# Starting the first expert pass with six early 256-token blocks

## The reference, cut to what matters

```python
scores = (jnp.einsum('btd,ed->bte', x, router_w) + router_b) / temp
gates = _sinkhorn(scores)
topk_vals, topk_idx = jax.lax.top_k(gates, K)
g = jax.nn.relu(jnp.einsum('btd,edf->btef', x, wg))
p = jnp.einsum('btd,edf->btef', x, wp)
all_out = jnp.einsum('btef,efd->bted', g * p, wo)
...
x = L0_attn_x
x = x + _L0_attn_ref(xn, ...) + _L0_ffn_ref(xn, ...)
```

## Time and profile before

| what | value |
|---|---|
| median of three runs | 388.4 us (387.77 to 388.95) |
| span of the profiled execution | 387.7 us |
| TensorE busy | 346.6 us |
| GpSimd busy | 267.4 us |
| mean granted TensorE clock | 0.982 |

### The profile page before, as it was taken

One profiled execution on the slowest core, in us unless ns is written; L12 is line 12 of the kernel. 1 busy time (PEld: TensorE's weight loads), 2 busy tenths in 40 slices (PEclk: granted clock), 3 DMA queues, 4 the chain that ended last, 5 costly groups with the idle time before them and its releaser, 6 DMA issues.

```text
span 387.7 us, 8994 instructions
## 1 busy us (share of the span) xinstructions
PE 346.6 (89%) x2632; PEld 311.0 (80%) x2632; DVE 271.5 (70%) x745; ACT 235.4 (61%) x442; POOL 267.4 (69%) x363
## 2 busy tenths in 40 slices
PE   0779799799989888999999999999999999999880
PEld 0769568667768777786699999999999999999770
DVE  3998789998798888774266666676656666666440
ACT  3679644126756655653268777777767777775530
POOL 3696999947877544647065777777756777777773
PEclk9999999969999999999999999999999999999996
DMA  6999999997424323259467677677674555563330
GB/s 181 253 315 334 336 334 266 319 248 225 137 100 146 116 82 98 94 157 310 112 170 191 191 214 210 183 223 212 174 207 116 160 135 164 140 170 106 93 103 0
DMA packets 64287, 70.98 MB, mean 183 GB/s; under 512 B 6099, under 2 KB 59103, under 8 KB 64241
## 3 DMA queue, kind: packets, MB, share of 16 engines
q1 hardware_dynamic: 53968, 48.56, 47.6%
q0 software_dynamic: 8672, 21.19, 15.0%
q10 hardware_dynamic: 1600, 0.67, 0.7%
HBM read 28.54 MB, written 43.04 MB: 185 GB/s over the span
## 4 chain that ended last, share of the span: by engine, by line
PE 68%; DVE 16%; issue 6%; POOL 4%; DMA 3%; ACT 2%; SPq 0%; ACTq 0%; POOLq 0%; DVEq 0%
PE psum L1652 15%; PE psum L1639 7%; PE psum L1640 7%; PE psum L1641 7%; PE psum L1617 4%; PE psum L1459 3%; PE psum L1521 3%; PE psum L1629 3%; POOL out L551 3%; PE psum L1350 2%; DVE stats L844 2%; PE psum L1441 2%; DMA rows<-in_L_attn_x 2%; PE psum L1403 2%; PE psum L1444 2%
## 5 line engine op out<-in xcount | busy, mean ns | idle before, releaser
L537 POOL DMA_INDIRECT by_upper<-row x70 | 69.0, 985 | 35.0 <-issue 15.1
L529 POOL DMA_INDIRECT by_lower<-rows,slot_u x64 | 64.5, 1008 | 36.0 <-DVE rows L960 19.2
L551 POOL DMA_INDIRECT out<-row x70 | 68.8, 983 | 25.7 <-issue 15.9
L1652 PE MATMUL psum<-w_expert,hT 128*128 x560 | 76.9, 277 | 1.0 <-DVE hT L1283 0.5
L1639 PE MATMUL psum<-xT_high,w_now 128*128 128x256 f32 x232 | 70.2, 303 | 0.8 <-issue 0.8
L1652 PEld LDWEIGHTS psum<-w_expert,hT 128*128 128x128 f32 x560 | 69.4, 192 | 1.8 <-issue 1.6
L748 ACT ACTIVATE w_now<-w_split 128x1024 fp32r x58 | 61.4, 1058 | 15.4 <-PE psum L1641 15.4
L1641 PE MATMUL psum<-xT_high,w_now 128*128 128x256 f32 x232 | 65.5, 282 | 0.0
L1640 PE MATMUL psum<-xT_low,w_now 128*128 128x256 f32 x232 | 65.4, 282 | 0.0
L1287 DVE TENSOR_TENSOR hT<-relu,psum 128x512 f32<-128x512 f32 x58 | 39.9, 687 | 34.7 <-PE psum L1641 31.3
L1295 DVE SCALAR_TENSOR_TENSOR row<-psum,row 128x128 f32<-128x128 f32 x140 | 43.6, 346 | 9.6 <-PE psum L1652 1.5
(11 more groups left out here) (256 smaller groups left out, 697.4 us busy)
## 6 DMA issues: line engine op xcount, KB each, us to landing
by_lower<-blank SPq DMA_DIRECT2D x1, 10140.0 KB, 34.8
by_upper<-blank SPq DMA_DIRECT2D x1, 10062.0 KB, 72.7
row<-by_lower SPq DMA_DIRECT2D x29, 260.0 KB, 3.4
row<-by_upper SPq DMA_DIRECT2D x29, 258.0 KB, 3.1
rows<-in_L_attn_x SPq DMA_DIRECT2D x8, 512.0 KB, 9.5
row<-by_upper SPq DMA_DIRECT2D x12, 129.0 KB, 2.2
row<-by_lower SPq DMA_DIRECT2D x11, 130.0 KB, 2.4
by_upper<-row POOLq DMA_INDIRECT x70
```

Source lines behind the costliest of these rows:

```text
L529: pool.indirect_dma_start(by_lower, bass.IndirectOffsetOnAxis(ap=slot_u[:, t:t + 1], axis=0), rows[:, t, :], None).then_inc(scattered, 16)
L537: pool.indirect_dma_start(by_upper, bass.IndirectOffsetOnAxis(ap=row[:, q, k, SLOT_UP:SLOT_UP + 1].bitcast(U32), axis=0), row[:, q, k, 0:R ...
L551: pool.indirect_dma_start(out_rows, bass.IndirectOffsetOnAxis(ap=row[:, q, k, TOKEN:TOKEN + 1].bitcast(U32), axis=0), row[:, q, k, BASE], ...
L1652: last = pe.matmul(psum[:, 4 + n % 2, k * D:(k + 1) * D], hT[:, n % 3, f, k * P:(k + 1) * P], weights, start=(f == 0), stop=(f == FB - 1))
```

## The change

Pass one starts with six pairs (LEAD = 6), then come the 12 singles, then the other 23 pairs. SP may load one of the six as soon as the scatters of the first 52 tiles (SOON) have landed, if the block lies wholly in them by a table (`lead_need` is 1), and otherwise when all 64 have (`lead_need` is 2). GpSimd counts this in the semaphore `arrived`. The table is computed on VectorE: three more instructions in `pair_bounds`, one in `class_bounds`, the new `lead_waits` of seven in iteration 10, one in `entry_numbers`. The ring changes places with w_whole, xT_low and relu, so that rows can be loaded during the attention's last groups and w_whole can't; SP's order is now: load_expert(1) to (6), six row loads, both copies of w_whole (once the last output chunk is through), the row loads 6 to 9, load_expert(7), the rest. The fillers go, round and divide of expert 6 stand before the attention's last instructions, those of expert 7 in blocks 20 and 21, and a register load is made for each word of packed numbers when it is first needed.

```diff
+    LEAD = 6
+    SOON = 52
+    FIRST_PASS = [*range(LEAD), *range(PAIRS, NE), *range(LEAD, PAIRS)]
+    def listed(n):
+        return FIRST_PASS[n] if n < NE else n - NE
     def width(n):
-        return 1 + ((n % NE >= SINGLES) if n < NE else (n % NE < PAIRS))
-    def listed(n):
-        return (n + PAIRS) % NE if n < NE else n - NE
+        return 1 + (listed(n) < PAIRS)
...
             w_now = last_use("w_now", [P, 2, 4 * FF], F32R)
-            w_whole = last_use("w_whole", [P, E, 2 * FF])
+            row = last_use("row", [P, NB, 2, ROW])
...
-        LAST_BANKS = (6, 7, 0, 1)
+        LAST_BANKS = (6, 7, 3, 4)
...
+        def pack_reader(engine):
+            packs = {}
+            def expert(a, i):
+                at = listed(a * NE + i)
+                k = a * NPACK + at // PACK
+                if k not in packs:
+                    _, (packs[k],) = nc.values_load_multi_w_load_instructions(packed_no[:, k:k + 1], ...)
+                return (packs[k] >> (3 * (at % PACK))) & (E - 1)
+            return expert
...  SP, load_row and the queue
                 if n == 0:
-                    sp.wait_ge(scattered, 16 * NT)
+                    sp.wait_ge(q_ready, NG - 1)
+                if n < LEAD:
+                    sp.wait_ge(arrived, sp.value_load(lead_need[:, n:n + 1], min_val=1, max_val=2))
+                if n == LEAD:
+                    sp.wait_ge(arrived, 2)
...
-            sp.wait_ge(q_ready, NG)
+            sp.wait_ge(route_dve, TABLES_STEP)
+            for n in range(LEAD):
+                load_row(n, by_lower, ROW)
+            sp.wait_ge(o_chunk, G)
             sp.dma_start(w_whole[:, :, 0:FF], wg.rearrange("e p f -> p e f")).then_inc(whole_loaded, 16)
             sp.dma_start(w_whole[:, :, FF:2 * FF], wp.rearrange("e p f -> p e f")).then_inc(whole_loaded, 16)
-            sp.wait_ge(o_chunk, G)
-            load_expert(E - 1)
-            sp.wait_ge(route_dve, TABLES_STEP)
-            for n in range(NE):
+            for n in range(LEAD, NE):
+                if n == LEAD + 4:
+                    load_expert(E - 1)
                 load_row(n, by_lower, ROW)
...  GpSimd
-                                            rows[:, t, :], None).then_inc(scattered, 16)
+                                            rows[:, t, :], None)\
+                        .then_inc(scattered_soon if t < SOON else scattered_late, 16)
+                    if t == SOON:
+                        pool.wait_ge(scattered_soon, 16 * SOON)
+                        pool.sem_inc(arrived, 1)
+            pool.wait_ge(scattered_late, 16 * (NT - SOON))
+            pool.sem_inc(arrived, 1)
...  ScalarE
-            round_expert(E - 2)
+                if n == NG - 2:
+                    round_expert(E - 2)
...
+                        if n + 4 == LEAD:
+                            act.wait_ge(whole_loaded, 32)
...  VectorE
+            def lead_waits():
+                soon_to = bounds[:, 2, 0]
+                link(dve.tensor_tensor(soon_len[:], soon_to[:, 1:], soon_to[:, 0:K], ALU.subtract))
+                link(dve.tensor_tensor(soon_end[:], pairs_to[:, 0, 0:K], soon_len[:], ALU.add))
+                link(dve.tensor_tensor(soon_more[:], soon_end[:, 1:], soon_end[:, 0:K - 1], ALU.subtract))
+                link(dve.tensor_tensor(lead_part[:], in_later[:, 0, 0:LEAD], soon_more[:]..., ALU.mult))
+                link(dve.tensor_reduce(lead_sum[:], lead_part[:], AX_X, ALU.add))
+                link(dve.scalar_tensor_tensor(lead_late[:], lead_sum[:], soon_end[:, 0:1], pair_at[:, 0:LEAD],
+                                              ALU.add, ALU.is_le))
+                link(dve.tensor_scalar(lead_need[:], lead_late[:], 1.0, None, ALU.add))
...
-                link(dve.tensor_scalar(need_no[:], need[:], pair_end[:, 0:1], float(SINGLES), ALU.add, ALU.add))
+                link(dve.tensor_scalar(need_first[:], need[:], pair_end[:, 0:1], float(LEAD), ALU.add, ALU.max))
+                link(dve.tensor_scalar(need_no[:], need_first[:], float(SINGLES), None, ALU.add))
...
+            divide_expert(E - 2)
             for c in range(G):
                 finish_last(c)
-            divide_expert(E - 2)
...  TensorE
-            unread(36)
-            pe.wait_ge(scattered, 16 * NT)
-            unread(13)
```

More of the change, by code:

```diff
@@ L171, in sparse_block_kernel @@
         before_wide = sb("before_wide", [K2, 2, K + 1])
-        wide = sb("wide", [K2, 2, 2, K + 1], BF16)
+        wide = sb("wide", [K2, 3, 2, K + 1], BF16)
+        soon_sum = sb("soon_sum", [K2, 1], I32)
+        soon_no = sb("soon_no", [K2, 1], I32)
+        soon_f = sb("soon_f", [K2, 1])
+        soon_len = sb("soon_len", [1, K])
+        soon_end = sb("soon_end", [1, K])
+        soon_more = sb("soon_more", [1, K - 1])
+        lead_part = sb("lead_part", [1, LEAD, K - 1])
+        lead_sum = sb("lead_sum", [1, LEAD])
+        lead_late = sb("lead_late", [1, LEAD])
+        lead_need = sb("lead_need", [1, LEAD], I32)
         pair_sum = sb("pair_sum", [K2, 1], I32)
@@ L235, in sparse_block_kernel @@
             rden = first("rden", [P, G])
-        row = sb("row", [P, NB, 2, ROW])
+        xT_low = sb("xT_low", [P, 2, W], F32R)
+        relu = sb("relu", [P, 2, FB * W])
         hT = sb("hT", [P, 3, FB, W])
+        w_whole = sb("w_whole", [P, E, 2 * FF])
         psum = ctx.enter_context(nc.psum_tensor("psum", [P, 8, 512], F32))
         x_in = [sem(f"x_in{b}") for b in range(B)]
-        (v_loaded, w_loaded, const_ready, lower_cleared, upper_cleared, scattered) = steps(
-            "v_loaded w_loaded const_ready lower_cleared upper_cleared scattered")
+        (v_loaded, w_loaded, const_ready, lower_cleared, upper_cleared, scattered_soon, scattered_late, arrived) = steps(
+            "v_loaded w_loaded const_ready lower_cleared upper_cleared scattered_soon scattered_late arrived")
         (rw_loaded, rw_pe, rw_step, w_scaled, w_summed, w_sum_saved, w_step) = steps(
@@ L337, in turn_of @@
             return n // NB + 1
-        def load_numbers(engine, ap, top):
-            _, numbers = nc.values_load_multi_w_load_instructions(
-                ap, engines=[engine], min_val=0, max_val=top, bass_reorder=False,
-                skip_runtime_bounds_check_because="eight class numbers below 8 in base 8")
-            return numbers
+        def pack_reader(engine):
[4 more added lines that the diff above has]
+                if k not in packs:
+                    _, (packs[k],) = nc.values_load_multi_w_load_instructions(
+                        packed_no[:, k:k + 1], engines=[engine], min_val=0, max_val=E ** PACK - 1, bass_reorder=False,
+                        skip_runtime_bounds_check_because="eight class numbers below 8 in base 8")
+                return (packs[k] >> (3 * (at % PACK))) & (E - 1)
+            return expert
         block = ctx.enter_context(nc.Block())
@@ L789, in _ @@
                     n = n0 + i
-                    if a == 0 and i == 6:
+                    if a == 0 and i == LEAD + 14:
                         round_expert(E - 1)
@@ L1235, in divide_expert @@
                    .then_inc(w_divided, 1)
-            TABLES = {5: class_lengths, 6: pair_places, 8: single_places, 9: choose_singles, 11: entry_numbers}
+            TABLES = {5: class_lengths, 6: pair_places, 8: single_places, 9: choose_singles, 10: lead_waits, 11: entry_numbers}
             for n in range(EARLY, NG):
@@ L1304, in _ @@
                     n = n0 + i
-                    if a == 0 and i == 7:
+                    if a == 0 and i == LEAD + 15:
                         divide_expert(E - 1)
@@ L1600, in _ @@
                 out_chunk(n, 3)
-            def unread(count):
-                for _ in range(count):
-                    pe.matmul(psum[:, 3, 0:K * NT], before_h[:], member[:, 0].rearrange("p k t -> p (k t)"),
-                              start=True, stop=True)
-            unread(36)
-            pe.wait_ge(scattered, 16 * NT)
-            unread(13)
             def turn_row(n):
@@ L1615, in turn_row @@
                     pe.wait_ge(xT_ready, n - 1)
+                else:
+                    pe.wait_ge(row_done, NT - G + n + 1)
                 for k in range(width(n)):
```

53 lines of the change are left out of this document (27 added, 26 removed).

## The result

| | before | after |
|---|---|---|
| median, us | 388.08 (385.73 to 388.95, 4 runs) | 383.02 (382.15 to 384.45, 4 runs) |
| profiled execution: own time, span | 388.4, 387.7 | 382.31, 379.9 |

The ratio is 0.988, with a 95% interval of 0.9845 to 0.9915: 5.1 us faster between the medians. 382.5 was forecast.

A forecast was written before the change was run, and what follows sets the result against it. GpSimd's series of scatters, 1.29 us each, was taken to set the end. Span 387.7 - 6.4 (earlier last pass-one scatter) + 0.5 (added instructions) = 381.8, with 0.7 for the median 382.5 us; range 378.4 to 384.8.

The forecast's parts named there:

- The bound: Both passes: GpSimd's scatters, 1.29 us each, set the end; it never waits in pass two.
- The six blocks: Row loads before pass one: all six lie wholly in 52 tiles, `lead_need` 1, rows issued from about 169 to 180.
- third rival: Row loads: table gives 2 for the first block, SP waits until 185.6, last scatter 3.4 us later; 392.3 us, chance 0.05.
- TensorE's start: First up product of pass one: at 180.8 instead of 189.18, 8.4 us gained.
- GpSimd's start, the deciding term: First pass-one scatter: last by_lower scatters land at 188.6 beside the 2 MB copy, start at 189.5, 4.0 us earlier.
- The copy itself: w_whole before the singles: second half takes 9.6 us, landed by 188.7, wanted by ScalarE at 191.7, 3 us in hand.
- The ring: Ten row slots in pass one: TensorE loses 3.1 us at block 15; GpSimd, done at 220.5, waits to about 222.5.
- The small things: Added VectorE instructions cost 0.5 us in all; split register loads nothing, or 3.2 us on TensorE if not covered.
- The first: Rival at GpSimd's start: scatters do not wait for w_whole, start at 186.4, 9.7 us won; 379.2 us, chance 0.23.
- The second: Rival: register loads not covered, added VectorE instructions all count, or the clock falls; 4.3 us won, 384.2 us, chance 0.13.
- Sum: Whole kernel: span 387.7 - 6.4 + 0.5 = 381.8, median 0.7 above the span, 382.5 us; chance 0.55.

The follow-up runs named there:

- E3: Changed kernel with its table forced to 2, so SP waits for all 64 scatters before the first row; 394.28 us, ratio 1.0167.
- E5: Kernel before the change without its fillers (49 products that nobody reads) and the wait on `scattered` between them; 390.14 us, ratio 1.005.
- E4: Changed kernel with 16 fillers, products that nobody reads, put back on TensorE before the first transposes; 382.25 us, ratio 0.9883.
- E1: Changed kernel with eight leading pairs instead of six (LEAD = 8), `w_whole` issued behind them; 384.98 us, ratio 0.9922.
- E2: Changed kernel with one semaphore for all 64 scatters; SP waits for 832 or 1024, GpSimd only for the first 52; 381.96 us, ratio 0.984.
- E6: E2 with the second megabyte of the whole weights issued only when all 64 scatters have landed; 385.3 us, ratio 0.9904.
- E7: Changed kernel with the second megabyte of the whole weights issued only after GpSimd has signalled all 64 scatters; 383.0 us, ratio 0.99.
- E8: Changed kernel with four leading pairs instead of six, the other two behind the singles; 384.88 us, ratio 0.9928.
- E12: E2's kernel on another chip, where the kernel before took 460.8 us; 463.05 us, ratio 1.005.

## Why the prediction was right

**The bound.** GpSimd's series sets the end: 1.29 us a tile, no gap after tile 24, pass two unchanged, and all of the gain is in its start. Right.

**The six blocks.** All needed 52 tiles alone: their rows were issued up to 177.09, before the last scatter. E3 shows what the other outcome costs: 394.3, where the prediction's third rival had 392.3. The rival's mechanism was right and its price 2 us short; it had no term for the clock, which cost about that in E5.

**TensorE's start.** Predicted 180.8; 179.16, aligned 180.92. E4 shows that it had 2.3 us to spare.

**GpSimd's start, the deciding term.** Predicted 189.5 from a last landing at 188.6; aligned 190.01. The hold of the scatters beside the 2 MB is shown by E1: take the copy away and the start is 185.24 instead of 188.25. The sum needed the upper part of the bounds, and got it for a reason that was only half right: the scatters did not wait for the copy's end (they had landed by 187.5, the copy at 190.1), the last four took 5.7 to 7.2 us instead of 2.5, and some 1.8 of that was there without the copy. The last landing was forecast for 188.6 and came at 187.3, aligned 189.05. The Trainium skill (DMA: Bandwidth & Descriptors, Queues, rings and completion order) has the engines take turns by packet between queues. The trace agrees in kind: a scatter is slowed, not locked out. But it would be wrong to read from it that the wait is nothing. The trace before could have told: counted by the packets of GpSimd's DMA queue, 48 for each of these scatters, the two issued at 170.1 and 171.3 beside the same copy were through only about 6 us after their issue, those before the copy and the last one about 2.1 (without the last 0.4 us to the semaphore).

**The copy itself** was the worst of the sizes: 9.6 us was taken for the second half, and it took 12.1. The prediction had 3 us in hand for ScalarE and got a wait of 0.69. ScalarE's need came when it was forecast: predicted 191.7, 189.97 in the trace, aligned 191.7.

**The ring.** Predicted to hold TensorE 3.1 us at block 15, and GpSimd to wait 2.0 (222.5 against 220.5). TensorE waited 2.9 us in 3 pieces for rows between 202 and 209, where it was forecast, and GpSimd 2.36 beyond its pace. That the ring is what held these rows is read from where the waits fall and from E2, in which GpSimd is earlier and only two waits of 0.7 are left; no run with another ring was made. The last scatter of the pass: predicted 280.6, aligned 281.38; 0.5 of the 0.8 came from the later start.

**The small things.** From group 3's score to group 15's it took 86.47 us before and 86.74 after, 0.27 for all the VectorE instructions that were added, where 0.5 was taken. Even this is not clear of the scatter of single traces: E5, which has none of them, took 86.65. The register loads cost nothing visible: the starts of pairs on TensorE stay 2.5 us apart. The pause between the passes was 4.16 instead of 4.61, which gave back 0.45.

**The other rivals.** The first (scatters not held, 379.2) did not come about, and E1 and E2 show that its price was wrong as well: with the start at 185.3 the time is 385.0 and 382.0. The step that fails in it is "block 18 is ready at 218.6 and GpSimd goes on at 219.2". It took TensorE to be unheld once GpSimd is early. In E2 TensorE still waits twice for rows, its row of block 18 is ready only at 219.6, and the 25th scatter starts at 220.42, aligned 222.0. The second did not come about: by the pairs' spacing the register loads were covered, the VectorE instructions cost 0.3 at most, and the clock did not fall. (Its own terms add up to 384.3 or 384.4, not 384.2.) The forecast itself was not touched by this, since 189.5 lies where TensorE is just ahead.

**Sum.** Aligned, the last start of pass one moved by 5.6 us instead of 6.4, the pause gave 0.45, and 0.3 of the 0.5 for the tables is in the 5.6 already: 6.05 in the two profiles, 5.9 between the medians of the spans, where 6.4 - 0.5 = 5.9 was forecast. The base was less good. The profiled execution's span of 387.7 is 1.6 us above the median of the spans (386.1), with the half-clock stretch in it, and its own time lies only 0.7 above its span. By medians the same working is 386.1 - 5.9 + 1.8 = 382.0, and with the 0.6 outside the span, which no step had, 382.6. That 382.5 is so near 383.02 is in part luck: two errors of the base cancel.

**A better version.** E2's ratio (0.984, 0.9806 to 0.9874) is below that of the changed kernel (0.988) and of E4 (0.9883), but the intervals overlap, and the profiles of E2 and the changed kernel differ by 0.2 us when aligned; it may be 1 us faster, which is not shown. No version here clearly beats the changed kernel.

## What to carry to other kernels

When one engine's gapless series sets the end, an earlier start pays only up to the point where its suppliers run level with it: compare the paces (1.49 against 1.29 here) before counting the whole shift. A large copy must be placed against two dates, what it holds up beside it and who wants it: E1 won 3 us at one and lost more at the other. A small load issued behind it on the same queue landed only after it (E6). In an engine's written order a wait for late data also stops the ready work behind it; look for that work before moving the wait, and where a view names a row as the releaser, check when that row was really ready.

## What the runs showed that was not expected

- 128-row scatters of 1 KB rows took 2.5 us to land alone (E3), 4.0 to 4.4 beside the early row loads, 5.7 to 7.2 beside the 2 MB copy as well and 5.0 to 7.1 beside the first 1 MB of it (E7); a 130 KB row load issued 1.5 us after a 1 MB copy on the same queue took 9.0 instead of 2.9 (E6).
- The granted clock fell to half not only after a long idle time: in E7 from 193.3 to 196.7, right after one wait of 1.87 us for a row, in E8 from 193.9 to 197.3 after one of 3.51, and in pass two of E2 from 357.6 to 361.0 after one of 2.24. In the changed kernel, with waits of 1.32 at 179 and 0.9 to 1.2 at 202 to 209, it did not fall.
- In the attention, the half-clock stretch near 80 is there in some executions and absent in others of the same code, and the time of group 3's score goes from 85.1 to 87.8 with it. Two single profiles should be aligned behind it before their spans are compared.
- On one chip the kernel before took 19% longer (460.8 against 388). In E12 beside E2, the same code, GpSimd, VectorE and ScalarE were busy as long as elsewhere to about 3 us, TensorE 27 us longer.
